# Row statistics moved into the gated stage, a transposition by VectorE through DRAM, and float32 dot products

## The reference

```python
xn = layernorm(x)
# random features (256 of them)
def rfs(xw):                       # ab = xis, AB = exp(xis)
    dot = xw @ (ab[:, None] * proj_matrix).T
    corr = 0.5 * (xw * xw).sum(-1)[..., None] * (ab * ab)
    return 1 / sqrt(256) * AB * exp(dot - corr)
s = rfs(xn) @ rfs(input_weights).T
# feed-forward, 256 -> 1024 -> 1024 -> 1024 -> 256
h = silu((xn @ w1.T) * w1_s) * ((xn @ w2.T) * w2_s)
h = gelu((h @ h1.T) * h1_s)
h = gelu((h @ h2.T) * h2_s)
g = silu((h @ w3.T) * w3_s)
out = x + s * g
```

## Time and profile before

| what | value |
|---|---|
| median of the runs | 1322.44 us |
| the profiled execution: time, span | 1323.1 us, 1321.3 us |
| PE busy | 1303.4 us (99%) |
| DVE, ACT, POOL busy | 944.0 us (71%), 755.0 us (57%), 592.4 us (45%) |
| TensorE clock granted (mean) | 0.999 |

### The profile page before, as it was taken

The page is one execution under the profiler, slowest core; times in us unless marked ns, Lnnn a source line. Parts: engine busy times, 40 slices in busy tenths (PEclk is TensorE's granted clock), DMA queues, the critical chain, the costliest instruction groups (busy, mean ns, idle before and its releaser), DMA issues.

```text
span 1321.3 us, 16508 instructions
## 1 busy us (share of the span) xinstructions
PE 1303.4 (99%) x6300; PEld 1103.7 (84%) x6300; DVE 944.0 (71%) x1205; ACT 755.0 (57%) x1016; POOL 592.4 (45%) x617
## 2 busy tenths in 40 slices
PE   7999999999999999999999999999999999999997
PEld 6878898888988888888888888888898888988887
DVE  7797866788658886688876676757766666675675
ACT  4456654666546665456654656555565565555664
POOL 5884968899688987889977000000000000000000
PEclk9999999999999999999999999999999999999999
DMA  9998841644516545255433444234451344514451
GB/s 254 295 329 280 278 114 71 204 155 148 128 69 199 169 123 129 91 189 166 118 122 118 154 143 91 102 128 136 152 116 61 131 156 137 119 48 143 131 165 42
DMA packets 98949, 194.94 MB, mean 148 GB/s; under 512 B 19120, under 2 KB 21424, under 8 KB 97840
## 3 DMA queue, kind: packets, MB, share of 16 engines
q1 hardware_dynamic: 86176, 157.11, 38.5%
q0 software_dynamic: 12688, 36.71, 9.1%
HBM read 168.58 MB, written 31.49 MB: 151 GB/s over the span
## 4 chain that ended last, share of the span: by engine, by line
PE 97%; DMA 1%; DVE 1%; ACT 0%; issue 0%; SPq 0%; DVEq 0%; ACTq 0%
PE ps L216 74%; PE ps L219 21%; PE ps L303 1%; DMA ring<-hs 1%; DMA quad<-in_win 1%; DVE split L199 0%; DVE ry L199 0%; DVE WS L204 0%; DVE xin L199 0%; ACT quad L195 0%; DVE quad L209 0%; PE ps L231 0%; DVE xT L199 0%; SPq L86 0%; ACT split L195 0%
## 5 line engine op out<-in xcount | busy, mean ns | idle before, releaser
L216 PE MATMUL ps<-split,ring 128*128 128x512 f32 x2800 | 764.2, 390 | 1.8 <-DVE split L199 1.4
L216 PEld LDWEIGHTS ps<-split,ring 128*128 128x128 f32 x2800 | 525.5, 188 | 111.9 <-DVE split L199 1.8
L199 DVE TENSOR_TENSOR split<-quad,split 128x1024 fp32r<-128x1024 f32 x258 | 335.8, 1309 | 184.7 <-ACT split L195 184.2
L195 ACT ACTIVATE split<-quad 128x1024 fp32r<-128x1024 f32 x258 | 267.2, 1052 | 72.4 <-PE ps L219 72.4
L219 PE MATMUL ps<-split,ring 128*128 128x512 f32 x784 | 305.0, 389 | 0.0
L216 PE MATMUL ps<-xT,w 128*128 128x512 f32 x768 | 216.3, 390 | 0.1
L547 POOL TENSOR_TENSOR cube<-cube,seen 128x256 f32<-128x256 f32 x176 | 191.0, 1085 | 14.3
L195 ACT ACTIVATE quad<-ps 128x512 f32<-128x512 f32 x192 | 114.6, 598 | 131.5 <-PE ps L219 131.4
L195 ACT ACTIVATE quad<-quad,cols 128x512 f32<-128x512 f32 (+1 forms) x194 | 139.4, 720 | 82.2 <-DVE quad L199 80.9
L199 DVE TENSOR_TENSOR quad<-quad 128x1024 f32<-128x1024 f32 x128 | 175.8, 1414 | 3.6 <-DMA hs<-quad 3.6
L219 PEld LDWEIGHTS ps<-split,ring 128*128 128x128 f32 x784 | 147.2, 188 | 30.5
(11 more groups left out here) (91 smaller groups left out, 1017.6 us busy)
## 6 DMA issues: line engine op xcount, KB each, us to landing
ring<-hs SPq DMA_DIRECT2D x428, 256.0 KB, 3.6
xin<-in_x SPq DMA_DIRECT2D x17, 512.0 KB, 7.6
s_h<-s SPq DMA_DIRECT2D x16, 512.0 KB, 2.6
seen<-in_h POOLq DMA_DIRECT2D x64, 128.0 KB, 2.9
ry<-in_x SPq DMA_DIRECT2D x15, 512.0 KB, 5.4
out<-ry SPq DMA_DIRECT2D x15, 512.0 KB, 2.6
hs<-in_h SPq DMA_DIRECT2D x6, 1024.0 KB, 8.5
ring<-in_h POOLq DMA_DIRECT2D x20, 256.0 KB, 6.8
```

Source lines behind the costliest of these rows:

```text
L195: return act.mark(lambda e: e.activation(dst, src, func, scale=scale))
L199: return dve.mark(lambda e: e.tensor_tensor(dst, a, b, op))
L216: pe.run(lambda e: e.matmul(dst, stat, mov, start=start, stop=stop, skip_group_check=loose))
```

## The change

- In tiles 1 to 6 the statistics and the normalisation stand in the gated stage of the tile, not in the product layers. The rows of the next tile are loaded at the start of the tile.
- The normalised rows of halves 4 to 15 are not turned by PE. POOL stores each half to DRAM in four DMAs that arrange blocks of 32x32 (`rows_out`: runs of 32 numbers), loads it back (`rows_in`), and DVE transposes the 32x32 blocks in two operations a half (`turn_blocks`), ahead of the third and fourth quarter of products 2 and 3 of L0; ACT and DVE then make the high and the low part (`split_rows`). Halves 0 to 3 are still turned by PE.
- `PT` is no longer split: `dots` is done with float32 matmuls on an unsplit copy of the turned rows (`xTf`, which lies in the buffer of `xin`), two for each block r; for t >= 1 it stands ahead of the gated stage. The same holds for the small products of the input weights at the start (`dots_win`).
- `gate_y` and `store_y`'s addition are done by POOL for halves 0 to 13.
- `count_good` is spread over tiles 1 to 6, 16 chunks each.
- The norms are stored as 128 runs of 4 numbers.

```diff
-            PT = sf("PT", [P, 2, KD, R], F32R)
+            PT = sf("PT", [P, KD, R])
...
-        q_h = nc.dram_tensor("q_h", [NH, NB, P], F32).ap()
+        q_h = nc.dram_tensor("q_h", [NH, P, NB], F32).ap()
+        z_h = nc.dram_tensor("z_h", [2, 4, 32, NB * KD, 4, 32], F32).ap()
...
+        def rows_out(h):
+            j = h % 2
+            pool.wait(xn_done[h, NB - 1], *([d_zin[j].token] if h - 2 in z_stored else []))
+            for c in range(4):
+                z_stored[h] = d_zout[j].send(pool, z_h[j][:, :, :, c, :].rearrange("a i n j -> i n a j"),
+                                             xin[j][32 * c:32 * c + 32, :, :].rearrange("i b (k a j) -> i (b k) a j", k=KD, a=4))
+
+        def rows_in(h):
+            j = h % 2
+            pool.wait(z_stored[h], *xT_free[h - 2])
+            d_zin[j].send(pool, xT[j][:, :, 1, :].bitcast(F32), z_h[j].rearrange("a i n c j -> (a i) (n c j)").rearrange("p (c t) -> p c t", c=2))
+
+        def turn_blocks(h):
+            j = h % 2
+            dve.wait(d_zin[j].token)
+            for kd in range(KD):
...
+                xTf_done[h] = dve.mark(lambda e, dst=dst, src=src: e.transpose(dst, src))
+            xT_hi[h] = cast(xT[j][:, :, 0, :], xTf[j][:, :, :], xTf_done[h], *xT_free[h - 2])
+
+        def split_rows(h):
+            j = h % 2
+            xT_lo[h] = vv(xT[j][:, :, 1, :], xTf[j][:, :, :], xT[j][:, :, 0, :].bitcast(F32), ALU.subtract, xT_hi[h])
...
-                pe.wait(xT_lo[h], *free[banks[r]])
-                tok = group(ps[:, banks[r], :], [(PT[:, wh, kd, r * P:(r + 1) * P], xT[j][:, kd, g, :])
-                                                 for kd in range(KD) for wh in range(2) for g in range(2)])
+                pe.wait(xTf_done[h], *free[banks[r]])
+                tok = group(ps[:, banks[r], :], [(PT[:, kd, r * P:(r + 1) * P], xTf[j][:, kd, :]) for kd in range(KD)])
...
+        def both_of(h, dst, a, b, op, *tokens):
+
+            if h >= 2 * NT - 2:
+                return vv(dst, a, b, op, *tokens)
+            pool.wait(*tokens)
+            return pool.mark(lambda e: e.tensor_tensor(dst, a, b, op))
...
-                side = {0: [lambda: silu_y(h0 - 1)], 1: [lambda: gate_y(h0 - 1)], 2: [lambda: store_y(h0 - 1)],
-                        3: [lambda: scale_y(h0 - 2), lambda: silu_y(h0 - 2)], 5: [lambda: gate_y(h0 - 2)], 6: [lambda: store_y(h0 - 2)]}
+                dots(h0, (4, 5), L0.at["v"])
+                dots(h1, (2, 3), L0.at["v"])
+                next_rows()
+                side = {0: [lambda: silu_y(h0 - 1), lambda: gate_y(h0 - 1), lambda: store_y(h0 - 1)],
+                        5: [lambda: scale_y(h0 - 2), lambda: silu_y(h0 - 2), lambda: gate_y(h0 - 2), lambda: store_y(h0 - 2)]}
+                for m, part in enumerate((todo[:1], todo[1:2], todo[2:3], todo[3:4], todo[4:6], todo[6:7])):
+                    side[m + 2] = side.get(m + 2, []) + part
...
+            side = {0: [split(L0, "b11", 0)], 1: [split(L0, "b11", 1)]}
+            if t == 0:
+                side[2], side[3] = [split(L0, "b21", 0)], [split(L0, "b21", 1)]
+            if 0 < t < NT - 1:
+                for m, part in enumerate((todo[7:8], todo[8:9], todo[9:10], todo[10:11] + rows_go[0], todo[11:12], todo[12:13] + rows_go[1][:1],
+                                          todo[13:14] + rows_go[1][1:])):
+                    side[m] = side.get(m, []) + part
...
+                for task in [split(L0, "b21", 0), split(L0, "b21", 1)] + sums[:2]:
...
+            if 0 < t < NT - 1:
+                for h in (h0 + 2, h1 + 2):
+                    rows_in(h)
+                for h in (h0 + 2, h1 + 2):
+                    norms_in(h)
+            if 0 < t < FLAG_TILE:
+                counted[0] = count_good(16)
...
+                (2, 0): [split(L0, "t1", 0)], (2, 1): [split(L0, "t1", 1)], (2, 2): [fill, fill] + later(turn_blocks, h0 + 2), (2, 3): [fill, fill] + later(split_rows, h0 + 2),
+                (3, 2): [fill, fill] + later(turn_blocks, h1 + 2), (3, 3): [fill, fill] + later(split_rows, h1 + 2),
...
-                if t + 1 < NT and n == 0:
+                if t == 0 and n == 0:
                     turn_rows(h0 + 2, (4, 5))
-                if t + 1 < NT and n == 2:
+                if t == 0 and n == 2:
                     turn_rows(h1 + 2, (6, 7))
```

More of the change, by code:

```diff
@@ L179, in build @@
         d_qout, d_qin = [port(f"d_qout{j}") for j in range(2)], [port(f"d_qin{j}") for j in range(2)]
+        d_zout, d_zin = [port(f"d_zout{j}") for j in range(2)], [port(f"d_zin{j}") for j in range(2)]
         q_stored = [None, None]
@@ L538, in factory, with count_good @@
             yt_free[:] = res_free[:] = [stored[1].token]
-        def count_good():
+        counted_chunks = [0]
+        def count_good(some):
             chunks = [w_kpm[n][:, k, c:c + COUNT] for n in ("h1", "h2", "w1", "w2", "w3")
@@ L547, in step @@
                 pool.wait(pool.mark(lambda e: e.tensor_tensor(dst, a, b, op)))
-            d_seen[0].send(pool, seen[0][:, :], chunks[0])
-            for n in range(len(chunks)):
+            first = counted_chunks[0]
+            last = counted_chunks[0] = min(first + some, len(chunks))
+            if first == 0:
+                d_seen[0].send(pool, seen[0][:, :], chunks[0])
+            for n in range(first, last):
                 if n + 1 < len(chunks):
@@ L578, in build @@
         a_ab = act.mark(lambda e: e.activation(amp[:, 0, :], xis, ACT.Exp))
[L580 removed]
+        PAIRS = [((6, 7), (4, 5), (2, 3), (0, 1))[n] for n in (0, 1, 2, 0, 1, 2, 0, 1, 3, 2, 0, 3, 1, 2, 3, 0)]
         PAIRS0 = [((6, 7), (4, 5), (2, 3))[n % 3] for n in range(2 * KH)]
@@ L605, in turn_proj @@
             two = ps[:, 2, :].rearrange("p (a b) -> p a b", a=2)
[L606 to L613, removed]
+            made_w["PT"] = cast(PT[:, :, :], two, tok)
+            free[2] = [made_w["PT"]]
+        wt = quad[5][:, 0, :].rearrange("p (a b) -> p a b", a=KD)
         def turn_win():
@@ L619, in turn_win @@
             two = ps[:, 3, :].rearrange("p (a b) -> p a b", a=2)
[L620 to L625, removed]
+            made_w["wt"] = cast(wt, two, tok)
+            free[3] = [made_w["wt"]]
         def norms_win():
@@ L648, in dots_win @@
             for r in range(KD):
-                tok = group(ps[:, 0, r * D:(r + 1) * D], [(PT[:, wh, kd, r * P:(r + 1) * P], F[:, kd, g, 0:D])
-                                                          for kd in range(KD) for wh in range(2) for g in range(2)])
-            f_free[:] = [tok]
+                tok = group(ps[:, 0, r * D:(r + 1) * D], [(PT[:, kd, r * P:(r + 1) * P], wt[:, kd, :]) for kd in range(KD)])
+            quad_free[5] = [tok]
             made_w["dots"] = tok
@@ L823, in build @@
         scale_proj()
-        rest_proj = turn_proj()
-        rest_win = turn_win()
+        turn_proj()
+        turn_win()
         for task in stats_tasks([0]):
             task()
-        rest_proj()
-        rest_win()
+        norms_win()
         turn_rows(0, (4, 5))
         dots_win()
-        norms_win()
         factory()
@@ L855, in sub, with next_rows @@
                 return lambda: L.subtract(name, g)
+            def next_rows():
+                for h in (h0 + 2, h1 + 2) if t + 1 < NT else (h0,):
+                    load_x(h)
+            rows_go = [lambda: rows_out(h0 + 2)], [lambda: rows_out(h1 + 2), lambda: norms_out(h0 + 2), lambda: norms_out(h1 + 2)]
+            todo = stats_tasks([h0 + 2, h1 + 2]) if t + 1 < NT else []
             if t == 0:
+                fills += todo
                 stats1 = stats_tasks([1])
@@ L874, in build, with later @@
                 norms_in(1)
-            dots(h0, (4, 5), L0.at["v"])
-            if t == 0:
+                dots(h0, (4, 5), L0.at["v"])
                 features_win()
[L878 to L882, removed]
-            def norms_away():
-                if t + 1 < NT:
-                    norms_out(h0 + 2)
-                    norms_out(h1 + 2)
+                dots(h1, (6, 7), L0.at["v"])
+            def later(f, h):
+                return [lambda: f(h)] if 0 < t < NT - 1 else []
+            def norms_away():
+                if t == 0:
+                    for h in (h0 + 2, h1 + 2):
+                        norms_out(h)
+                    for h in (h0 + 2, h1 + 2):
+                        norms_in(h)
             sums = [sub(L0, n, g) for n in ("t1", "t2") for g in range(2)]
             if t:
-                for task in sums:
+                for task in [split(L0, "b21", 0), split(L0, "b21", 1)] + sums[:2]:
                     task()
```

44 lines of the change are left out of this document (23 added, 21 removed).

## The result

The changed kernel took 1315.52 us (median of five runs, 1313.97 to 1315.81), beside it the kernel before 1321.2: a ratio of 0.9944 over all runs, 95% interval 0.9922 to 0.9966 (the two medians alone give 0.9957). It is faster by 0.56%, where 12.5 us (0.95%) and a time of 1311 us were forecast. The profiled execution took 1315.81 us, 7.3 less than the one before.

What follows compares the result with a forecast made beforehand. PE, busy 99% of the span, was taken to bound the kernel. Transpositions (9.5 us) and dots (3.0) made 12.5 off 1323.1, 1310.6; half a microsecond for waits gave 1311, 8-in-10 range 1306 to 1350.

Steps and rivals of the forecast that it cites:

- PE's list: PE in all tiles: 9.5 us less from twelve halves' transpositions, 3.0 less from dots, 12.5 together; steady tile about 159.8 us.
- DVE in the gated stage: DVE's work there becomes 22.1 of 29 us; it falls 2 us behind, 3 with POOL active, but stays narrowly hidden.
- cover of 3.6: Gated stage: rotating PSUM banks let DVE be two PE steps, 3.6 us, late before PE waits.
- first rival: Gated stage stalls: DVE over 3.6 us behind, PE waits 1 to 3 us a tile, six times; 1317 to 1329, chance 0.16.
- likeliest case: Whole kernel: PE's smaller gain comes through and other work stays hidden; 1307 to 1315 us, chance 0.58.
- The start: Tile 0, beside half 0's normalisation: fewer dots_win matmuls and DVE subtractions, norms_win moved earlier; nothing, within 1 us either way.
- Loads of x: Next tile's rows land 7.6 us after request, at 11 and 14.5 us into the tile; barely hidden.
- Stores: Normalised halves through DRAM: second lands at 30 + 2X + 6.4 us, needed by about 71; hidden up to X = 17.
- X: Time in us to store one normalised half to DRAM; taken as 11, with 2.6 and 47 as ends of its range.
- The rival of late stores: DVE waits at second half's `turn_blocks`; beyond X = 17 each microsecond costs 2 a tile, 1343 to 1667; chance 0.19.
- signs of being wrong: New profile would show DVE or PE waits, late ring loads beside the stores, or counting running into the next tile.
- POOL: POOL's work takes 127 to 133 of about 160 us a tile; hidden. Its rival, 1341, shares chance 0.07 with others.

## Why the prediction was right, and where not

*PE's list.* Right. Dots take 0.86 us a matmul, 6.86 a tile; alone they brought 3.7 us for the 3 forecast. A half's transpositions cost 0.86 for the 0.79. The steady tile with the waits removed takes 159.75 to 159.80 us; 159.8 was forecast. PE's instructions fell from 6300 to 6068, the transposition matmuls from 128 to 32.

*DVE in the gated stage: "Hidden, narrowly."* This step failed. The sum over the stage was 22.1, and the trace has DVE busy 24.75 us (21.02 before); with POOL's operations left out it is 22.85, so the list itself was nearly right. The places were named rightly (split, small operations and gating at the first steps of the second half). The size of what POOL does to DVE was wrong: taken as a share (a split 1.39 instead of 1.22), while in fact one operation stands until POOL's has ended, 1.8 to 2.4 us at a time. In the prediction's own terms POOL was to put DVE 1 us further behind, 3 us against a cover of 3.6; one hold puts it 1.6 to 2.2 behind, and with the 2 of DVE's own list that is 3.6 to 4.2, past the cover. It cost 6.1 us in six tiles. That is the mechanism of the first rival at its lower end (1 us a tile); the time, 1315.5, lies between the likeliest case's own range (to 1315) and that rival's (from 1317).

The sentence on the rule of the Trainium skill ("SBUF — State Buffer", on the two separate sides), by which a split behind an addition of POOL could wait 2.6 us, was nearer than the row. The wait came whole, until POOL's operation ended. In tile 7 it met a split, as that sentence has it (3.40 us for 1.21), and cost nothing there. In tiles 1 to 6, where it cost time, it met a small operation: in tiles 2 and 4 to 6 one with two inputs in SBUF, in tiles 1 and 3 one with a single input (`TENSOR_SCALAR` at 525.94), of which that sentence says nothing. The gating, which reads PSUM, was not held (0.75 us at 523.87, while POOL's gate ran from 523.26).

*DVE's work moved to POOL.* Not weighed as a term of its own. Without it the change, in this order of work, would be slower than before (1328.03). The normalisation, forecast at 8.4 us a tile, measures 7.3 (22.85 less 15.59 in the run without POOL's operations).

*The start: "I put it at nothing, within 1 us either way", and of the norms' store "shortens that DMA; SP's queue had time already".* The number held by luck, and the reason failed: the start won 1.4 us, tile 0 lost 3.7 ahead of mix and won 2.5 between mix and down, which comes to about 0.3 won. That store had been delaying POOL, and so kept POOL out of DVE's way; faster, it let POOL start at 20.43 instead of 25.69 (before first, then after, and one of the small operations of DVE that POOL then held, 0.16 us otherwise):

```profile
25.69 2.75 POOL L505 TENSOR_TENSOR s<-s 128x512 f32<-128x512 f32 x2 [4.20 <-DMA s<-in_h]
```

```profile
20.43 5.50 POOL L535 TENSOR_TENSOR s<-s 128x512 f32<-128x512 f32 x4
```

```profile
20.52 1.32 DVE L211 SCALAR_TENSOR_TENSOR sm<-sm 128x4 f32<-128x4 f32 x1
```

The same earlier start took POOL's weight sums out of L0's way, which gave the 2.5 us back. No step had foreseen either.

*Loads of x.* Hidden as said, with more room: 3.2 us to land for 7.6, no wait.

*Stores.* Hidden, as forecast. In tile 4 the eight issues of two halves begin at 697.70, and POOL goes on at 712.38, when they have landed: 7.3 us a half, for X = 11 taken.

```profile
697.70 8.17 POOL L86 DMA_DIRECT2D z_h<-xin  x8 [5.63 <-DVE xin L207]
...
712.38 0.73 POOL L86 DMA_DIRECT2D xT<-z_h  x1 [5.68 <-DMA z_h<-xin]
```

The rows land some 55 us into the tile, 16 ahead of the limit. The 11 rested on a misreading: the 1,056 short packets are the norms' own 1,024 runs (all of 4 B in the trace), so that 11 us and 47 us came from one and the same store. The rival of late stores stays untested at its own place, DVE at `turn_blocks`: at three times the stores X was (760.74 - 725.82) / 2 = 17.5, just past its point of 17, but the kernel became far slower through the ring's loads, which the prediction has only among its signs of being wrong, and the clock, and PE's waits for the ring came first. The 512 B that the Trainium skill wants ("DMA: Bandwidth & Descriptors", Specifications) did not decide: at 128 B a half's 512 KB stored in 7.3 us, nearer to the 2.6 of long runs than to 47.

*POOL.* A gate or addition takes 2.39 to 2.41 us, once 3.34; forecast 2.6 to 3.9. POOL idles 14.67 us ahead of the gate of tiles 3 to 6, 9.75 in tile 2. It is not the limit.

## What to carry to other kernels

Before work goes to GpSimd, ask which small operations of VectorE on SBUF will stand next to it: price each as one whole GpSimd operation, not as a percentage. A stage where VectorE fits on average still stalls when its slack, here less than 2.3 us, is shorter than one such hold; moving 2.4 us of other work out of the stage repaired it (0.9911). A slow transfer can keep an engine out of another's way, so a faster one has a price that only the order of work shows.

## What had not been expected of the hardware

- An operation of VectorE on 128x8 numbers in SBUF, even one with a single input, lasts until the GpSimd operation that it meets has ended: 2.25 us for 0.17. A split of 128x1024 took 3.40 us for 1.21.
- The store of 512 numbers in runs of 4 B delayed 512 KB loads on other queues: 11.0 us to landing with it, 5.7 with 128 runs.
- Extra stores of 128 B runs filled the 16 DMA engines (0.99 to 1.01) and delayed loads on another queue by up to 4.3 us at a matmul, 27.5 us in all; in a stretch of 10 us with 4.6 us of such waits TensorE's granted clock was 0.67, and 0.82 in the next (1.00 is 2.4 GHz, the lower level 1.2).
